# A Mamba2 scan with routed experts on one core: the softplus steps spread out, the first and last tiles reordered, the decayed inputs made after the masked product

## The reference, cut to what matters

```python
xn = _layernorm(x)                                  # 2048 tokens x 512
x = x + mamba2(xn) + moe(xn)

zxbcdt = xn @ in_proj_w.T                           # z, x, B, C: 2304 columns, and 16 of dt
dt = softplus(zxbcdt[..., -16:] + dt_bias)
xBC = silu(conv_b + sum(conv_w[:, k] * shifted(xBC, k) for k in range(4)))
dA_cs = cumsum(-exp(A_log) * dt)                    # within a chunk, for each of 16 heads
Y_diag = (C @ B.T * tril(exp(dA_cs[l] - dA_cs[s]))) @ (x * dt)
states = B.T @ (exp(dA_cs[-1] - dA_cs) * x * dt)
prev = scan(carry * exp(dA_cs[-1]) + states)
Y_off = (C @ prev) * exp(dA_cs)
y = rmsnorm((Y_diag + Y_off + x * D_skip) * silu(z)) @ out_proj_w.T
# moe: scores of 8 experts, the best two a token, softmax of the two,
# silu(x @ gate) * (x @ up) @ down, weighted and added
```

## Time and profile before

| | |
|---|---|
| median of 3 runs | 737.36 us (736.17 to 737.4) |
| the profiled execution, its own time | 735.81 us |
| its span in the profile | 734.0 us |
| PE, DVE, ACT, POOL busy | 647.0, 531.2, 374.4, 311.2 us |
| mean granted TensorE clock | 0.967 of full |

### The profile page before, as it was taken

The page is one execution under the profiler, slowest core; times in us unless marked ns, Lnnn a source line. Parts: engine busy times, 40 slices in busy tenths (PEclk is TensorE's granted clock), DMA queues, the critical chain, the costliest instruction groups (busy, mean ns, idle before and its releaser), DMA issues.

```text
span 734.0 us, 12653 instructions
## 1 busy us (share of the span) xinstructions
PE 647.0 (88%) x4189; PEld 530.3 (72%) x4190; DVE 531.2 (72%) x1116; ACT 374.4 (51%) x787; POOL 311.2 (42%) x223
## 2 busy tenths in 40 slices
PE   4857899999999999999999989884868999999992
PEld 3747778768777786777877868563547889989981
DVE  4966879977987997996998798877947744444430
ACT  3673963763754566366376373636035644444441
POOL 1110335353444452543535325245434666565642
PEclk9979999999999999999999999998878999999996
DMA  8830304032230430421403303095086577677663
GB/s 258 327 134 31 115 1 145 30 115 89 86 116 30 144 117 5 153 99 34 144 31 116 115 2 115 1 229 145 5 287 189 96 135 134 124 122 129 121 100 43
DMA packets 32050, 80.91 MB, mean 110 GB/s; under 512 B 4800, under 2 KB 10048, under 8 KB 29824
## 3 DMA queue, kind: packets, MB, share of 16 engines
q1 hardware_dynamic: 22176, 55.22, 22.6%
q0 software_dynamic: 9056, 21.50, 16.2%
q10 hardware_dynamic: 768, 3.54, 2.0%
HBM read 60.45 MB, written 19.79 MB: 109 GB/s over the span
## 4 chain that ended last, share of the span: by engine, by line
PE 41%; DVE 34%; issue 9%; ACT 5%; POOL 4%; DMA 4%; SPq 0%; DVEq 0%; POOLq 0%; ACTq 0%
PE pg L1610 11%; DVE xs L916 7%; PE pi L1419 7%; PE pd L1623 7%; PE po L1458 6%; DVE y L1196 3%; DVE step_acc L884 3%; PE py L1496 2%; DMA e<-cs_d 2%; PE px L1593 2%; PE py L1503 2%; DVE carry L1294 2%; DVE xs L931 2%; POOL ln L461 2%; ACT m L647 1%
## 5 line engine op out<-in xcount | busy, mean ns | idle before, releaser
L1419 PE MATMUL pi<-xh,whl 128*128 128x256 f32 x1152 | 167.2, 288 | 8.1 <-DVE zs L922 7.2
L1419 PEld LDWEIGHTS pi<-xh,whl 128*128 128x128 f32 x1152 | 148.3, 191 | 12.4 <-issue 11.1
L1458 PE MATMUL po<-wo,y 128*128 128x512 f32 x256 | 116.0, 607 | 8.1 <-DVE cbm L1219 8.1
L916 DVE SCALAR_TENSOR_TENSOR xs<-raw,conv_w,xs 128x256 f32<-128x256 f32 x240 | 112.5, 534 | 11.6 <-ACT xs L622 11.6
L1458 PEld LDWEIGHTS po<-wo,y 128*128 128x128 f32 x256 | 48.5, 194 | 64.0 <-issue 55.3
L1419 PE MATMUL pi<-xl,whl 128*128 128x256 f32 x576 | 92.2, 282 | 0.0
L531 POOL DMA_INDIRECT out<-yo,idx x39 | 62.0, 1590 | 56.5 <-ACT yo L776 31.8
L647 ACT ACTIVATE m<-m,cs_tok 128x128 f32<-128x128 f32 x256 | 79.7, 389 | 0.5
L1419 PEld LDWEIGHTS pi<-xl,whl 128*128 128x128 f32 x576 | 79.0, 190 | 0.0
L506 POOL TENSOR_TENSOR carry<-carry,cd 128x1024 f32<-128x1024 f32 x15 | 29.0, 1932 | 90.4 <-PE py L1496 90.4
L1610 PE MATMUL pg<-ew,xgh 128*128 x312 | 66.6, 357 | 0.7 <-issue 0.7
(11 more groups left out here) (203 smaller groups left out, 1200.1 us busy)
## 6 DMA issues: line engine op xcount, KB each, us to landing
m<-cs_d SPq DMA_DIRECT2D x16, 1024.0 KB, 5.6
e<-cs_d SPq DMA_DIRECT2D x32, 256.0 KB, 4.8
w_as_read<-in_w_in SPq DMA_DIRECT2D x9, 512.0 KB, 7.6
res<-in_x SPq DMA_DIRECT2D x16, 256.0 KB, 2.7
out<-o SPq DMA_DIRECT2D x16, 256.0 KB, 2.0
ew<-in_w_gu SPq DMA_DIRECT2D x5, 768.0 KB, 8.3
xin<-in_x SPq DMA_DIRECT2D x6, 512.0 KB, 3.4
xn_d<-xin SPq DMA_DIRECT2D x6, 512.0 KB, 2.8
```

The costliest lines, as they stand in the source:

```text
L916: dve.scalar_tensor_tensor(out=xs[par][:, b, :], in0=raw[:, b, k:k + GT], scalar=conv_w[:, b, k:k + 1], in1=xs[par][:, b, :], op0=ALU.mult ...
L1419: mm = pe.matmul(bank[:, hf, :], whl[:, weight(g, n), lo, k, hf * P:(hf + 1) * P], xx[:, k, :], start=k3 == 0, stop=k3 == 11)
L1458: mm = pe.matmul(po[:, :], y[:, b, :], wo[:, b, :], start=b == 0, stop=b == XB - 1)
```

## The change

Three kinds of edit, all of order; no instruction is added or taken out, and no buffer changes.

1. GpSimd's `xdd` waits for `m_done` (VectorE's masked product of the same tile) in place of `xdt_done`.
2. The softplus steps of the odd tile are taken as 0 to 9 between the two halves of `decayed`, 10 to 13 before the second `own`, 14 to 17 at the tile's end; they were 0 to 1, 2 to 4, 5 to 7, 8 to 10, 11 to 17.
3. Head and last tiles: ScalarE's decays of tile 0 move behind the router, gate and weight work, and TensorE's stage 5 behind the product C B; the squares and variance of the tile before move behind `diag(0)` and `own(0)` in tiles 14 and 15; the table products 0, 3, 4 move from the end of tile 14 into tile 15; the splits of expert 0 move out of tile 15; squares(15) on TensorE moves behind `gate_up(0)`, variance(15) and finish(15) on VectorE behind the splits of experts 0 to 3.

```diff
@@ -489,7 +489,7 @@
...
                 if t < T - 1:
-                    pool.wait_ge(xdt_done, 2 * t + 2)
+                    pool.wait_ge(m_done, t + 1)
                     pool.wait_ge(dec_done, t + 1)
@@ -684,19 +684,16 @@
...
             group_high(1)
+            stage(0, 4)
+            weight_high(6)
+            router_rows(1)
+            gated(0, NX - 1)
+            scores(1)
             decay_factors(0)
             kernel_part(0, 0, 4)
-            stage(0, 4)
-            kernel_part(0, 1, 4)
-            router_rows(1)
-            gated(0, NX - 1)
-            kernel_part(0, 2, 4)
-            scores(1)
-            weight_high(6)
             step_exp(1)
             weight_high(7)
-            kernel_part(0, 3, 4)
-            weight_high(8)
+            kernel_part(0, 1, 4)
 
@@ -719,7 +716,11 @@
...
                 if t == 0:
-                    for n in range(NX, NP):
+                    weight_high(8)
+                    stage(0, 5)
+                    kernel_part(0, 2, 4)
+                    kernel_part(0, 3, 4)
+                    for n in range(NX + 1, NP):
                         stage(0, n)
@@ -789,10 +790,10 @@
...
             down_high(act, 2)
+            square(T - 1)
             high(0, 0)
...
             gate_up_high(act, 3)
-            square(T - 1)
             gate_up_high(act, 4)
@@ -1163,10 +1164,10 @@
...
             group_low(1)
-            decay_differences(0)
             stage(0, 4)
...
             gated(0, NX - 1)
+            decay_differences(0)
             time_steps(1, 0, 2)
@@ -1229,7 +1230,8 @@
...
                 if t == T - 1:
-                    table_given(5)
+                    for n in (0, 3, 4, 5):
+                        table_given(n)
                     table_place(1)
@@ -1263,27 +1265,27 @@
...
                     experts_of_tiles()
-                    gate_up_low(dve, 0)
-                    down_low(dve, 0)
                     table()
...
                 if c == 1 and prepares:
-                    time_steps(g + 2, 0, 2)
+                    time_steps(g + 2, 0, 10)
                 if c == 0 and prepares:
...
                 decayed(1)
-                if t:
+                if 0 < t < T - 2:
                     variance(t - 1)
                 own(0)
+                if t >= T - 2:
+                    variance(t - 1)
                 for n in taken[2:3]:
...
                 if c == 1 and prepares:
-                    time_steps(g + 2, 2, 5)
+                    time_steps(g + 2, 10, 14)
                 own(1)
@@ -1293,19 +1295,12 @@
...
                                       ALU.add).then_inc(cadd, 1)
-                if c == 1 and prepares:
-                    time_steps(g + 2, 5, 8)
-                if t == T - 2:
-                    for n in (0, 3, 4):
-                        table_given(n)
                 for n in taken[3:4]:
                     stage(g + 1, n)
-                if c == 1 and prepares:
-                    time_steps(g + 2, 8, 11)
                 for n in taken[4:]:
...
                 if c == 1 and prepares:
-                    time_steps(g + 2, 11, 18)
+                    time_steps(g + 2, 14, 18)
 
@@ -1331,15 +1326,16 @@
...
 
-            gate_up_low(dve, 1)
+            gate_up_low(dve, 0)
             low(0, 0)
             low(1, 1)
-            down_low(dve, 1)
+            down_low(dve, 0)
+            for e in (1, 2):
+                gate_up_low(dve, e)
+                down_low(dve, e)
+            gate_up_low(dve, 3)
             variance(T - 1)
             finish(T - 1)
-            gate_up_low(dve, 2)
-            down_low(dve, 2)
-            gate_up_low(dve, 3)
             gate_up_low(dve, 4)
@@ -1517,9 +1513,7 @@
...
                     tr.then_inc(xtr, 1)
-                if t == 0:
-                    stage(0, 5)
-                else:
+                if t:
                     stages(0)
@@ -1530,9 +1524,8 @@
...
                 if t == 0:
-                    stage(0, 6)
-                    stage(0, 7)
-                    stage(0, 8)
+                    for n in range(NX, NP):
+                        stage(0, n)
                     stages(0)
@@ -1556,12 +1549,14 @@
...
                 off(1)
-                if t:
+                if 0 < t < T - 2:
                     if c == 0 and g + 1 < G:
...
                 diag(0)
+                if t >= T - 2:
+                    squares(t - 1)
                 if t == T - 1:
@@ -1662,8 +1657,8 @@
...
             project(T - 1)
+            gate_up(0, 0, expert_of(0))
             squares(T - 1)
-            gate_up(0, 0, expert_of(0))
             for j in range(9):
```

## The result

| | median of 20 runs | range | ratio (95% interval) |
|---|---|---|---|
| before | 737.24 us | 732.17 to 739.62 | |
| after | 744.07 us | 738.66 to 746.77 | 1.0097 (1.0080 to 1.0114) |

The change makes the kernel slower by 1.0%, 7.1 us by the ratio (the medians are 6.8 apart). Forecast were +0.9 us and a range that ends at 742.8: the time lies outside it. The profiled executions are 735.81 and 744.89 us, spans 734.0 and 743.1, 9.1 apart; mean granted clock 0.967 and 0.945.

The account below looks back on a forecast made before the run. Neither TensorE (41%) nor VectorE (34%) was taken to own the launch; the end passes between them. Terms +2.5 +0.5 +3.5 -0.3 -5.3 = +0.9 us gave 738.3 on the runs' scale, range 733.8 to 742.8.

Parts of the forecast that it names:

- The wait in the even tile: Even tiles: `xdd` ahead of GpSimd's power makes VectorE's `normalise` start 2.7 us behind the masked product; net +1.75 us.
- The softplus: Odd tile: ten softplus steps fit VectorE's 3.14 us gap, bringing TensorE's next stage forward; gain 1.1 us per pair.
- the second blocked step: Odd tile, VectorE: another softplus step blocked by GpSimd, taken as similar to 1.40 us, which the new order avoids.
- +0.7: Tiles 2, 4, 6, 8, 10: even-tile cost 1.75 less softplus gain 1.1, rounded up; five times, +3.5 us.
- Rival (a): Stage 5 and tiles 14, 15: TensorE at 1.2 GHz and the lock take the tail's gain; 742.3 us, chance 0.22.
- the head: Start of the kernel: later second gate tanh and `xdd` blocking softplus steps +2.5 us, TensorE's clock in stage 5 +0.5.
- The block by `xdd`: Head: `xdd` starts at the masked product's end, and the thirteen softplus steps behind it wait 1.94 us.
- the tail: Tiles 14, 15 and the expert part's start: earlier gather and projection, first `hg` at 549.7; gain 5.3 us.
- the gathers then meet the loads of expert weights: +1: Expert part's start: the gathers, forecast 2.3 us earlier, meet expert weight loads, costing 1 us.
- Tiles 12 and 13: Softplus gain 1.1 in tile 12, +0.4 there from blocking, +0.4 late Y_off in tile 13; together -0.3 us.
- xdd in the odd tile: Odd tile: less blocking of the masked product, more of the multiply-adds; net 0, hidden under TensorE.
- Rival (b): Head and tail: VectorE's instructions slip through before `xdd`, so GpSimd waits instead; 734.7 us, chance 0.25.

Follow-up runs that it names:

- filling the wait: Whole change, with TensorE making the products of off(0) three times over in even tiles 2 to 10, against the kernel before: ratio 1.0059.
- The two parts alone: Two kernels on the kernel before: only the head reordered, ratio 1.0036; only the wait of `xdd` changed to `m_done`, ratio 1.0148.
- the kernel that held the loads: Kernel before plus the edit inside tiles 14 and 15, SyncE holding all that follows until the first two gathers land: ratio 1.0069.
- the early head: Kernel before with the head reordered and ScalarE making tile 0's last eight relu's and exponential ahead of the first gate tanh: ratio 0.9982.
- both edits together: Kernel before with the wait of `xdd` and the softplus steps changed, head and tail as before: 743.69 against 736.28 us, ratio 1.0084.
- xdd's wait alone: Kernel before with only the wait of `xdd` changed, `m_done` in place of `xdt_done`: 746.60 against 734.91 us, ratio 1.0148.
- the odd tiles' kernel: Whole change, but `xdd` waits for the masked product only in odd tiles and the last four, against the kernel before: ratio 0.9921.
- softplus with tail and hold: Kernel before with softplus spread, tail reordered, loads of experts 3 and 4 held until two gathers land: 724.08 against 734.07 us.
- the power taken first: Whole change, but GpSimd takes the layernorm power ahead of `xdd` in even tiles, against the kernel before: ratio 1.0016.

## Why the prediction was wrong, point by point

**The wait in the even tile** was right: 2.61 us for `ln`, and +1.75 a pair forecast, 1.3 to 1.9 measured alone at full clock. **The softplus** was right in kind and small in size: it fits the gap, and gives 1.5 a pair and 2.3 more in tiles 12 and 13, where the forecast had 1.1. (It also took the second blocked step to be similar to the 1.40; in the trace of before it is 2.26, at 297.01.)

**What failed first** is the step that adds the two to "+0.7" for each pair. In tile 4, the one without a half-clock stretch, the pair costs +0.6, as forecast. In the four others it costs 1.3 to 2.0. The prediction saw that TensorE would wait and that its clock falls after a wait; it had the row for it, 2.91 us of waiting and twice the normal time for eight matmuls. It applied that row to tiles 12 and 13, and priced the new wait in tiles 2 to 10 at the wait alone, with nothing for the clock. From `carry` of tile 0 to tile 11 the profiled executions moved by +7.1 where +3.5 was forecast, and filling the wait takes 4.9 of that away. Rival (a), the clock, named the right mechanism at the wrong places, and its 742.3 was 1.8 short.

**Second, the head**: forecast +3.0, and +6.7 at `carry` of tile 0. The two parts alone bring `carry` of tile 0 to 90.8 each. But some 2 us of either is no effect: kernels whose head and xdd's wait are untouched have it at 88.7 to 89.5 where the profiled execution of before has 87.2. Theirs have half the clock until 51.6 to 53.5, where it ended at 50.3, and again for 3.4 us from a point between 65.2 and 67.2, where in the trace of before it stayed up. The effect is thus about 4.7. The masked product of tile 0 starts at 61.66, against 59.1 to 59.8 in those kernels: some 2 us from the relu's between the gate pieces, not 0.6. Stage 5 started at 49.08, as forecast, but ran at 1.2 GHz throughout, so that the first gate tanh came at 54.5, and the 4.4 us behind it could not end by 57.2. The block by `xdd` cost 1.6 of the forecast 1.9 (at 64.17), and the last 1 us lies behind stage (1, 0), whose wait of 4.47 us is followed by half the clock until 74.7.

**Third, the tail**: forecast -5.3, worth nothing alone (interval 0 to +2 us). The order at the start of the expert part gave 3.9, the splits of expert 0 that it takes out of tile 15 among it. The half inside the tiles cost 4.5: "the gathers then meet the loads of expert weights: +1" is the mis-sized term, 1.4 us on the first rows and 4.3 on the second. That these late rows are the whole 4.5 is not shown, since the kernel that held the loads met another wait. Whether the first gather came the forecast 2.3 earlier cannot be read from single profiles: it stands 49.2 us behind `carry` of tile 13 in this half alone, and 47.6 to 52.7 in kernels with the old order of the tail. Between the two profiles the tail still seems to gain (13.4 to 9.0, 4.4 us). Scatter of this size needs no change there: with the tail untouched, the stretch from `carry` of tile 13 to the first `hg` took 76.4 us in the profile of before, 73.7 with the head alone and 71.8 with the early head. **Tiles 12 and 13** came out at -0.4 where -0.3 was forecast, but by luck: tile 12 moved by -3.3 and tile 13 by +2.9.

**xdd in the odd tile** cost nothing, as forecast. The port also behaved as the rows said: a blocked step 1.82, a blocked `normalise` 2.60. Rival (b), VectorE keeping the port, did not happen in any of these rows. The Trainium skill, "SBUF — State Buffer", section "Who interferes with whom", says that whoever has the shared pair of ports keeps it for the whole instruction and the other stands still. Those two rows agree: each lost 1.6 us beside an instruction of 1.93 that had begun just before. For the sums of squares the rows' price held and not the whole 2.8: in tile 6 the sums are 2.7 long and the twelve multiply-adds beside them take 6.54, 1.7 over the 4.83 that they take alone.

## What to carry to other kernels

Price a new wait of TensorE twice: once for its length, and once for the matmuls behind it at half the clock, where the trace has a row of that; and price edits that bear on one wait together, since a gain ahead of a wait can make it one long pause behind which the clock falls. Before moving work earlier on one engine, look which queue's transfers it sets free, and what lands next to them. Take a stage's length from several executions or several kernels that share it, not from one: here an untouched stretch varied by 4.6 us.

## What the hardware showed that was not expected

- In the even tiles 2 to 10 of all the kernels there were thirteen waits for `e` of 1.79 to 2.66 us (after and both edits together five each, one each in xdd's wait alone, the odd tiles' kernel, and softplus with tail and hold). Behind eleven the clock fell to 1.2 GHz for 3.4 us; behind one of 1.83 (tile 4 of after) and one of 2.25 (below) it did not. Behind the nine waits of 1.33 to 1.51 us of xdd's wait alone and of the power taken first it did not fall once. So the length of the wait alone does not settle it, and what else does stays open.

```profile
316.88 1.16 PE L1493 MATMUL py<-xs,carry 128*128 128x128 f32 x8 [2.25 <-DVE e L1188]
```

- Matmuls without use made the kernel faster: 1.7 us more of them in each of five tiles, 2.8 us less in all (0.6 to 5.0).
- Two gathers with a store, a load and the weights queued 0.5 to 1.3 us behind the first took 5.0 and 8.7 us to land, and 3.7 us with them held.
- With the period at 58 us, single tiles waited longer for the decays' loads: 6.25 and 5.84 us in tile 8 of two kernels, where the even tiles 2 to 10 otherwise show 2.5 to 4.4. What delays them was not tried and stays open.
